# Writing the overlapping key windows by DMA instead of by ScalarE, in a one-core attention and channel-mix kernel

## What is computed

```python
x = L0_attn_x                                  # (1, 4096, 256) f32
q = (x @ Wq + bq)   # 16 heads of 16, in 4 groups;  k, v: 4 groups of 16
scores = einsum('bghqd,bgkd->bghqk', q, k) / sqrt(16)
mask = (i - 128 >= j) | (i < j)                # each query sees itself and the 127 keys before it
att = softmax(where(mask, -1e9, scores));  a = (att @ v) @ Wo + bo
x = layernorm(x + a)
x_prev = shift x by one token
r = sigmoid((mu_r*x + (1-mu_r)*x_prev) @ W_r.T)
k = (mu_k*x + (1-mu_k)*x_prev) @ W_k.T
out = layernorm(x + r * (relu(k)**2 @ W_v.T))
```

## Time and profile before

| | |
|---|---|
| median of 3 runs | 394.36 us (394.3 to 394.94) |
| the profiled execution's own time | 395.03 us |
| its span (first to last instruction) | 393.3 us |
| mean granted TensorE clock | 0.966 of 2.4 GHz |
| busy PE, ACT, DVE, POOL | 366.5, 339.0, 328.4, 290.9 us |

### The profile page before, as it was taken

The page is one execution under the profiler, slowest core; times in us unless marked ns, Lnnn a source line. Parts: engine busy times, 40 slices in busy tenths (PEclk is TensorE's granted clock), DMA queues, the critical chain, the costliest instruction groups (busy, mean ns, idle before and its releaser), DMA issues.

```text
span 393.3 us, 8154 instructions
## 1 busy us (share of the span) xinstructions
PE 366.5 (93%) x2334; PEld 230.3 (59%) x2334; DVE 328.4 (83%) x860; ACT 339.0 (86%) x697; POOL 290.9 (74%) x485
## 2 busy tenths in 40 slices
PE   8666899999999999999999999999999998998984
PEld 5243346666566666666566666665666665665562
DVE  6257778999899989999899989999899988997654
ACT  4246999999999999999999999999999998986743
POOL 4704677887698778987698768887699777778633
PEclk9958699999999999999999999999999999999988
DMA  7745577622955247632954257531773262000001
GB/s 267 156 118 117 119 206 169 116 41 56 187 136 80 75 77 183 109 65 52 182 141 96 54 98 182 92 88 34 125 152 82 55 111 39 16 15 18 27 15 40
DMA packets 51244, 39.24 MB, mean 100 GB/s; under 512 B 33088, under 2 KB 42880, under 8 KB 51072
## 3 DMA queue, kind: packets, MB, share of 16 engines
q1 hardware_dynamic: 50480, 37.01, 43.7%
q10 hardware_dynamic: 720, 1.71, 1.6%
HBM read 26.38 MB, written 12.06 MB: 98 GB/s over the span
## 4 chain that ended last, share of the span: by engine, by line
PE 64%; ACT 20%; DMA 6%; issue 4%; DVE 3%; SPq 2%; POOL 1%; ACTq 0%; POOLq 0%; DVEq 0%
PE av_ps L1324 14%; PE score_ps L1304 10%; PE gen L1343 8%; PE gen L1414 7%; PE proj_ps L1221 6%; PE max_ps L1286 6%; ACT probs L696 6%; PE gen L1401 3%; PE gen L1384 3%; ACT windows L711 2%; ACT x L731 2%; DMA qs<-q_parts 2%; ACT out_t L769 2%; PE av_ps L1359 2%; ACT act_k L761 2%
## 5 line engine op out<-in xcount | busy, mean ns | idle before, releaser
L510 POOL TENSOR_SCALAR_AFFINE_SELECT probs<-probs 128x512 f32<-128x512 f32 x252 | 165.0, 671 | 52.0 <-ACT probs L696 50.9
L696 ACT ACTIVATE probs<-score_ps 128x512 f32<-128x512 f32 x252 | 142.6, 593 | 14.1 <-PE score_ps L1304 13.2
L965 DVE TENSOR_REDUCE neg_max<-max_ps 128x3 f32<-128x480 f32 x146 | 88.9, 631 | 12.2 <-PE max_ps L1286 11.9
L1304 PE MATMUL score_ps<-qs,ks 98*128 98x512 bf16 x252 | 87.9, 389 | 4.3 <-ACT probs L696 3.1
L711 ACT COPY windows<-ks 96x640 bf16<-96x640 bf16 x124 | 86.9, 727 | 4.8 <-DMA ks<-k_parts 4.8
L1324 PE MATMUL av_ps<-probs,vals 128*32 128x512 f32 x488 | 59.9, 606 | 0.0
L1006 DVE SCALAR_TENSOR_TENSOR mix<-diff,first,x_t 128x128 f32<-128x128 f32 x128 | 52.5, 453 | 2.9 <-POOL diff L538 2.6
L1286 PE MATMUL max_ps<-windows,q_tiles 128*128 128x160 bf16 x420 | 51.8, 239 | 1.0 <-DVE neg_max L965 0.9
L1286 PEld LDWEIGHTS max_ps<-windows,q_tiles 128*128 128x128 bf16 x420 | 36.4, 100 | 20.8 <-issue 3.7
L1304 PEld LDWEIGHTS score_ps<-qs,ks 98*128 98x128 bf16 x252 | 21.4, 98 | 39.9 <-issue 29.5
L517 POOL TENSOR_TENSOR rstd<-var,minus_half 128x1 f32<-128x1 f32 x64 | 35.4, 553 | 10.8 <-DVE var L989 10.7
(11 more groups left out here) (112 smaller groups left out, 612.0 us busy)
## 6 DMA issues: line engine op xcount, KB each, us to landing
q_parts<-parts SPq DMA_DIRECT2D x42, 128.0 KB, 2.2
out<-out_t SPq DMA_DIRECT2D x32, 128.0 KB, 2.4
qs<-q_parts SPq DMA_DIRECT2D x7, 576.0 KB, 6.9
x_t<-x_feat SPq DMA_DIRECT2D x7, 512.0 KB, 9.3
x_in<-x_nat SPq DMA_DIRECT2D x7, 512.0 KB, 3.8
ks<-k_parts SPq DMA_DIRECT2D x42, 80.0 KB, 3.2
qs<-q_parts SPq DMA_DIRECT2D x8, 384.0 KB, 8.0
qs<-q_parts SPq DMA_DIRECT2D x14, 192.0 KB, 5.9
```

The costliest lines, as they stand in the source:

```text
L510: nc.gpsimd.affine_select(out=v, in_=v, compare_op=ALU.is_ge if i % 2 else ALU.is_gt, fill=0.0, base=0, pattern=[[0, HPG], [sign, BLK]], c ...
L696: nc.scalar.activation(probs[:, buf, i], score_ps[i % 2][:, :], ACT.Exp, scale=SCALE).then_inc(s_exp, 1)
L965: nc.vector.tensor_reduce(neg_max[:, TPB * i:TPB * i + n], max_bank(t, j, i)[:, 0:n * TILE_KEYS].rearrange("p (n k) -> p n k", k=TILE_KEYS ...
L1304: nc.tensor.matmul(score_ps[i % 2][:, :].rearrange("p (h q) -> p h q", q=BLK), ks[0:ROWS + MPARTS, par, g, k0:k0 + BLK], qs[0:ROWS + MPART ...
```

## The change

Four edits are in it.

1. The windows of blocks 2 to 31 are written by SP: `window_load` issues four DMAs for a block, each 96 rows x 4 tiles x 160 keys (320 bytes a piece), from `ks` in SBUF to `windows` in SBUF. It stands first in SP's step (behind `load_x` where there is one) and waits for the same two counters as the ACT copy did: the key stack is there, and the maxima of the block that used this buffer are done. `max_scores` waits for the DMAs. ACT has no window copies left but the four of blocks 0 and 1.
2. Of the six head DMAs that stack the keys, three are issued by SP and three by ACT, on ACT ahead of the three for the queries.
3. ACT issues `first_rows` (x_in for superblock 0, 512 KB) after the window copies of blocks 0 and 1, not before; POOL's two first `x_plus_bo` move from its `start()` to the end of step 0, ahead of the two `low_part`s there. ACT's `high_part(1, 0)` moves ahead of the window copies of block 0.
4. On PE, `project_chunk(1, 2)` and `v_turn(1)` move ahead of the row maxima of block 0, with a second group of six fillers.

```diff
@@ SP
-                for r in range(NREP):
+                for r in range(NREP // 2):
                     sp.dma_start(ks[r * DH:(r + 1) * DH, 0, :, WINDOW:WINDOW + HEAD * BLK], ...
+            def window_load(t, s, j, par):
+                if t == HEAD or j == 0:
+                    sp.wait_ge(s_stack_k, s * K_STACKS + K_STACKS)
+                sp.wait_ge(s_maxsc, (t - 1) * NMAXB)
+                sp.nop(nofuse=True)
+                for g in range(GROUPS):
+                    src = ks[0:ROWS, par, g, j * BLK:j * BLK + TILE_KEYS]
+                    (lanes, rows), (k_step, _) = src.ap
+                    sp.dma_start(windows[0:ROWS, j % 2, g],
+                                 bass.AP(src.tensor, src.offset, [[lanes, rows], [k_step * SUB, NSUB], [k_step, TILE_KEYS]])
+                                 ).then_inc(s_window_d[t % 2], 16)
@@ SP step
                 ahead = project and later(s, 1)
+                if maxima and (project or j < SB_BLKS - 2):
+                    window_load(t + 2, s if j < SB_BLKS - 2 else s + 1, *at(j, par, 2))
                 if ahead and j == 0:
                     spill_k(s + 1)
@@ POOL start, step
-                x_plus_bo(0)
                 low_part(1, 0)
-                x_plus_bo(1)
...
                 if s == 0 and j == 0:
+                    x_plus_bo(0)
+                    x_plus_bo(1)
                     low_part(1, 1)
@@ ACT start
+            def head_stack_k():
+                act.wait_ge(h_spill_k, 16)
+                for r in range(NREP // 2, NREP):
+                    act.dma_start(ks[r * DH:(r + 1) * DH, 0, :, WINDOW:WINDOW + HEAD * BLK], ...
...
+                head_stack_k()
                 head_stack_q()
                 high_part(0, 2, max_ps[1])
                 middle_part(0, 1)
                 middle_part(0, 2)
-                first_rows()
+                high_part(1, 0, gen0)
                 window_copy(0, 0, 0, 0, 0)
                 window_copy(0, 0, 0, 0, 1)
-                high_part(1, 0, gen0)
                 high_part(1, 1, gen1)
                 window_copy(1, 0, 1, 0, 0)
                 window_copy(1, 0, 1, 0, 1)
+                first_rows()
@@ ACT step
-                if more:
-                    window_copy(t + 2, s2, j2, p2, 0)
...
-                if more:
-                    window_copy(t + 2, s2, j2, p2, 1)
-                    window_copy(t + 2, s2, j2, p2, 2)
...
-                if more:
-                    window_copy(t + 2, s2, j2, p2, 3)
@@ PE max_scores, start
-                        pe.wait_ge(s_window, (t + 1) * WINDOW_OPS - WINDOW_OPS)
+                        pe.wait_ge(s_window_d[t % 2], t // 2 * 16 * GROUPS)
...
                 project_chunk(1, 1, 1, gen1)
+                project_chunk(1, 2, 1, av_ps)
+                keep_running(score_ps[0], 6)
+                v_turn(1)
                 keep_running(score_ps[0], 6)
                 max_scores(0, 0, 0, 0)
...
-                project_chunk(1, 2, 1, av_ps)
-                v_turn(1)
```

More of the change, by code:

```diff
@@ L200, in attention_channel_mix @@
         s_window = sem("s_window")
+        s_window_d = [sem(f"s_window_d{i}") for i in range(2)]
         s_window_v = sem("s_window_v")
@@ L698, in window_copy @@
             def window_copy(t, s, j, par, half):
-                if half == 0:
-                    if t == 0:
-                        act.wait_ge(s_zero, 1)
-                        act.wait_ge(h_stack_k, K_STACKS)
-                    elif t == HEAD or j == 0:
-                        act.wait_ge(s_stack_k, s * K_STACKS + K_STACKS)
-                    if later(t, 2):
-                        act.wait_ge(s_maxsc, (t - 1) * NMAXB)
+                if half == 0 and t == 0:
+                    act.wait_ge(s_zero, 1)
+                    act.wait_ge(h_stack_k, K_STACKS)
                 g, n = GROUPS // WINDOW_OPS * half, GROUPS // WINDOW_OPS
@@ L770, in second_norm @@
                                      scale=rstd2[u % 2][:, 0:1]).then_inc(s_out, 1)
+            def head_stack_k():
+                act.wait_ge(h_spill_k, 16)
+                for r in range(NREP // 2, NREP):
+                    act.dma_start(ks[r * DH:(r + 1) * DH, 0, :, WINDOW:WINDOW + HEAD * BLK],
+                                  k_dram[K_PART[r], :, head].rearrange("(g d) t -> d g t", d=DH)).then_inc(h_stack_k, 16)
             def head_stack_q():
@@ L816, in step @@
                 f1, f2, f3, f5 = (behind(t, j, scores, n) for n in (1, 2, 3, 5))
-                more = maxima and (project or j < SB_BLKS - 2)
-                s2 = s if j < SB_BLKS - 2 else s + 1
-                j2, p2 = at(j, par, 2)
                 if ahead and j == 0:
                     middle_part(s + 1, 1)
-                if more:
-                    window_copy(t + 2, s2, j2, p2, 0)
                 if coming and j == 3:
```

## The result

The changed kernel took 405.75 us (402.51 to 411.06, 4 runs), the kernel before 394.65 us (394.3 to 396.65, 4 runs) in the same comparison. The ratio is 1.023, with a 95% interval of 1.019 to 1.027: slower, on the side to which I had given 0.21, and beyond the range's upper end. The profiled execution is the fastest of the changed kernel, 402.51 us, so what the trace explains is 7.4 us of span (400.7 against 393.3); what its other executions lost beyond that has no profile.

The account below looks back on a forecast made before the run. PE was taken to bound the kernel, losing a few tenths a step to ACT. Middle -6.5, steps 0 and 1 -1.5, start -1.8, DMA price +3.0 gave -6.8 us against 395.03: 388.2, or 387.5 on the median; range 380 to 396.5.

Parts of the forecast that it names:

- What bounds the kernel: Middle of the kernel: PE, busy 43.67 of 43.80 us, sets the pace and loses a few tenths a step to ACT.
- The term for the middle, -6.5: Blocks 2 to 31: window copies off ACT win 6.5 us, from their 2.5% of the chain; bounds 0 and 13.
- my 8: Gain from ACT's relief: 6.5 us for the middle and 1.5 us for steps 0 and 1.
- one of my signs of being wrong: Middle: the forecast is wrong if steps keep 10.95 us without a DMA wait.
- The price, +3.0: Window DMAs behind x_t in step j = 3: PE stands 0.6 us, in five superblocks, 3.0 us; bounds 0 and 15.
- about 1 us of slack: Step 1: windows come after the second query spill and have about 1 us to spare.
- a sign of being wrong: Maxima of j = 0: the forecast is wrong if PE's idle time before them is over 2 us.
- the maxima hidden: Maxima queued behind the windows in step j = 3: hidden, or 1 to 2 us late if the cover is gone.
- The start, -1.8: Start: block 0's maxima 0.95 us sooner at 22.0, clock 0.5, projection move 0.3; together 1.8 us, bounds 0 and 5.
- The 0.5 for the clock: Start, 20 to 30 us: fillers and projection cut PE's wait and the half-clock time, winning 0.5 us.
- The rival on the slower side: PE's first maxima of j = 0 or 2: windows arrive late and the kernel is slower, 399 us at 54.5 ns; chance 0.21.
- its turning point: Five such places: the change turns to a loss at 2 us each, 3.8 us a block or 40 ns a piece.

Follow-up runs that it names:

- e4: Kernel before without ACT's window copies of blocks 2 to 31 and nothing in their place, maxima taken over old windows; 389.68 us, ratio 0.986.
- e7: Kernel before, ACT's copies kept, plus the 120 window DMAs at the change's places, written to a spare tensor nobody reads; 404.31 us, ratio 1.016.
- e6: Kernel before with edits 2 to 4 alone, ACT copying all windows as before; 394.0 us, ratio 0.998.
- e12: e11 with six PE fillers behind block 0's maxima and two ahead of each score of step 0; 396.62 us, ratio 1.004 to the kernel before.
- e5: Kernel before with the first edit alone: windows of blocks 2 to 31 by SP, start as before; 405.93 us, ratio 1.027.
- e2: Changed kernel with SP issuing the windows ahead of x in steps j = 3; 400.87 us, ratio 1.012 to the kernel before.
- e14: Kernel before plus 120 DMAs of the same bytes to a spare tensor at the change's places, in pieces of 1280 bytes; 401.53 us, ratio 1.018.
- e15: Kernel before plus the 320-byte window DMAs to a spare tensor, issued at the end of SP's step; 401.45 us, ratio 1.017.
- e11: Kernel before with edits 2 to 4, block 2's windows copied in ACT's start, and DMA windows for nine blocks; 393.32 us, ratio 0.994.
- e9: Kernel before with windows by DMA for nine blocks only (7, 11, ..., 27 and 29, 30, 31), others by ACT; 395.76 us, ratio 1.000.
- e17: e7 with superblock 2's x issued in SP's start and superblock 1's rows one step later; 400.31 us, ratio 1.013 to the kernel before.

## Why the prediction was wrong

- **What bounds the kernel: right, and I drew too little from it.** PE was the bound, with pairs of 0.41 to 0.43 us after the change in all but the last blocks. The term for the middle, -6.5, was the chain's share of ACT's copies (2.5%), 1.1 us a superblock. In e4, of four steps, one falls by 0.29 us and one by 0.23, two not at all: 0.5 a superblock. So this term was about twice too large in the middle; e4 gives 5 to 6 us for the middle, the first steps and the end together, against my 8. A chain's share on an engine tells what ended a wait; here about half of it was not won. It nearly met one of my signs of being wrong: in the changed kernel the two superblocks from 233.69 to 321.23 us took 10.9 and 11.0 us a step, where I had put 10.7, and no wait of PE in them was over 0.3 us.
- **The price, +3.0: the step that failed.** Between e4, which has ACT's relief and no DMAs, and the changed kernel lie 13.0 us of span (387.7 to 400.7). I costed one place, the windows behind x at 5 superblock ends, at 0.6 us. It was there, but 1.4 to 1.6 us at three of them, and 0.15 and nothing at the two others. I had the piece right (25 ns against 23.9) and the turn: packets of the windows from 8.5 us after x's issue, where I had 8.8, to 11.3, where I had 11.2. PE wanted them at 11.0 after it, as forecast. What was too small is the rest, "a few tenths more to the semaphore": from the last packet to PE's start it was 1.2 us.
- **Superblock 0, costed at nothing: the largest miss, +6.6 us.** The text costs the windows that steps 0 and 1 issue ("about 1 us of slack") and stops there; it doesn't read the end of SP's step j = 1 of superblock 0, where `load_x(2, 0)` and `load_rows(1, 1)` issue 1 MB just ahead of step 2's windows. In this kernel's order the windows' place there is like that at the superblock ends, with twice the bytes. PE's idle time there, 3.42 us, is over the 2 us that I had named as a sign of being wrong. The rule that I gave for j = 3 (what stands ahead in the queue, and when does it land?) was not applied to every place where `window_load` stands. Behind the stall the granted clock stood at 0.50 for 6.8 us; this cost 2.1 us, which I had not counted anywhere.
- **What stands behind the windows.** I called the maxima hidden, and late by 1 to 2 us if the cover is gone. e7 shows the second: about 6 us with no one waiting for a window. And I put SP's issues at 0.47 us each, 1.9 a step, "which waits for the maxima most of the time"; they took 0.65 each and 3.2 us in e7's step 2, and held the maxima for 2.0 us there. This term stood at nothing in the sum.
- **The start, -1.8.** Block 0's maxima began at 22.87 us, not 22.0 (22.95 before). ACT waited 2.74 us for the spilled keys at 19.77, near the late end of my range for them. e6, the start's edits alone, gives nothing that can be told from no change (0.998, 0.996 to 1.001). The 0.5 for the clock has no run that shows it, and in e12 a higher clock in the start brought nothing.
- **The rival on the slower side** named the right mechanism and the right place among others, and its turning point, 2 us at each of five places, was not reached there (1.5 at three). It missed superblock 0. And its cause was wrong: it hung on the price of a piece (40 ns), while pieces stayed at 24 ns and their place and company made the wait. That it named the right side was in part luck. Transfers under 512 bytes do a read-modify-write by the Trainium skill ("DMA: Bandwidth & Descriptors", "Specifications"); the doubling that the prediction weighed from it did not show, as a piece of 320 bytes inside SBUF took 24 ns by the page of the profile. (Doubled, 25 ns would have been 50, past the turning point of 40 and not at it.)

Shown: the loss is the first edit's (e5, e6), the superblock ends are the x ahead of the windows (e2), PE's 3.4 us in superblock 0 are a wait for windows that landed late, and the DMAs cost 6 to 7 us without a waiter (e7, e14, e15). Only argued: how much of this price is SP's time at the issues, how much the place in the queue and how much the bytes; no run issues the windows from another engine, which would part the first from the rest. Open: why executions of the same kernel differ by several us (402.5 to 407.1 in the changed kernel), and why like orders land the maxima up to 3 us apart (e7 and e15, e11 and e12).

## What to carry to other kernels

A copy moved from an engine to the DMA queue must be costed at every place where it is issued: list what is issued in the 10 us ahead of it and behind it, the odd first round of the loop included, and not only its mean share. The time at the issues counts too, for what stands behind them in the issuing engine. Before that, find out what the relief is worth by the steps: leave the copies out and see which steps get shorter. Moving only those cut the loss here, but by itself it won nothing (e9, ratio 1.000). And transfers that no one waits for are not free when small urgent ones share their queue.

## What the runs showed of the hardware

- Pieces of 320 bytes inside SBUF took 24 ns each on an engine; for the same bytes pieces of 1280 took a fifth less of the engines' time, 56.5 against 71.9 us of 16 engines (e7, e14).
- PE started 1.2 and 1.0 us behind the last packet of the windows that it waited for, in full stretches (changed kernel).
- SP's issue of four such DMAs took 2.7 to 2.8 us at most places, and 4.10 and 4.84 (changed kernel) and 5.17 (e17) right behind an x_t: SP was held at the issue, and all behind it with it.
- With PE's granted clock at 0.82 in place of 0.50 over 12 us the first value product came no sooner (e12): 41.1 us against 41.0.
